# A transformer block on one core: the prologue reordered, token rows fetched ahead of expert results in the first pass

## What is computed

```
x = x + 0.5 * ffn(layernorm(x))
x = x + attn(layernorm(x))
x = x + 0.5 * ffn(layernorm(x))

ffn:  logits = t @ Wr.T + br; the two best of 8 experts; w = softmax of the two
      y = sum over the two of w * (relu(t @ W1[e].T + b1[e]) @ W2[e].T + b2[e])   # 128 -> 512 -> 128
      return layer_norm(t + y) * gamma + beta
attn: two score matrices per batch (q1 k1, q2 k2), out = (softmax(a1) - lam * softmax(a2)) @ v, then an RMS norm
```

## Time and profile before

| | |
|---|---|
| Time, median of 3 runs | 673.51 us (673.51 to 674.44) |
| The profiled execution's own time | 678.22 us |
| Its span in the trace | 676.5 us |
| TensorE busy | 596.4 us (88%) |
| VectorE, ScalarE, GpSimd busy | 452.3, 442.0, 389.7 us |
| Mean granted TensorE clock | 0.941 |

### The profile page before, as it was taken

How to read it: one execution, slowest core, us unless ns; L and a number is a source line. 1 busy time by engine, 2 the same in 40 slices (tenths; PEclk the granted TensorE clock), 3 DMA queues, 4 the chain that set the end, 5 groups by cost and what they waited for, 6 DMA issues and landing times.

```text
span 676.5 us, 16511 instructions
## 1 busy us (share of the span) xinstructions
PE 596.4 (88%) x4362; PEld 547.9 (81%) x4362; DVE 452.3 (67%) x1421; ACT 442.0 (65%) x1146; POOL 389.7 (58%) x481
## 2 busy tenths in 40 slices
PE   5988999999988759799989799897999978999945
PEld 5877999998988648688778689777999968998912
DVE  4775787445763838879968968986547553477635
ACT  4755666766656456686886786685776644887724
POOL 3006565557667178558633477585577777655623
PEclk9588999999987979999999999998999997999968
DMA  8902223223233011010000000021322423521051
GB/s 248 318 1 63 76 72 76 80 68 87 69 70 64 23 27 29 9 24 24 16 1 1 2 29 28 16 68 30 68 75 80 104 76 84 201 87 40 31 188 63
DMA packets 41881, 45.96 MB, mean 68 GB/s; under 512 B 8726, under 2 KB 32706, under 8 KB 41536
## 3 DMA queue, kind: packets, MB, share of 16 engines
q1 hardware_dynamic: 32496, 27.13, 13.7%
q0 software_dynamic: 9088, 17.75, 9.5%
q10 hardware_dynamic: 208, 0.02, 0.0%
HBM read 25.95 MB, written 19.83 MB: 68 GB/s over the span
## 4 chain that ended last, share of the span: by engine, by line
PE 53%; DVE 19%; issue 9%; POOL 8%; ACT 6%; DMA 4%; ACTq 0%; DVEq 0%; SPq 0%; POOLq 0%
PE banks L1061 18%; PE banks L1071 17%; DVE nb L1824 5%; DVE scratch L1831 3%; PE banks L1054 2%; PE banks L1158 2%; PE banks L949 2%; POOL zb L506 2%; PE banks L951 2%; PE banks L950 2%; DMA scratch<-xrows,rowbuf 2%; POOL rs L474 1%; DVE st_r L1321 1%; POOL rows L493 1%; DVE mv L1327 1%
## 5 line engine op out<-in xcount | busy, mean ns | idle before, releaser
L1061 PE MATMUL banks<-scratch 128*128 128x128 f32 x1248 | 172.9, 283 | 2.0 <-ACT scratch L695 1.0
L1071 PE MATMUL banks<-blocks,scratch 128*128 x1248 | 168.7, 279 | 3.1 <-ACT scratch L702 2.4
L1574 DVE TENSOR_SCALAR scratch<-banks,blocks 128x128 f32<-128x128 f32 x312 | 95.1, 346 | 107.4 <-PE banks L1061 97.3
L1061 PEld LDWEIGHTS banks<-scratch 128*128 128x128 f32 x1248 | 158.2, 199 | 5.5 <-issue 5.1
L1071 PEld LDWEIGHTS banks<-blocks,scratch 128*128 128x128 f32 x1248 | 154.4, 195 | 4.9 <-issue 4.5
L485 POOL DMA_INDIRECT scratch<-xrows,rowbuf x78 | 75.1, 963 | 82.0 <-DVE rowbuf L1469 42.7
L689 ACT ACTIVATE scratch<-banks 128x128 f32<-128x128 f32 x156 | 43.3, 277 | 110.1 <-PE banks L1054 108.2
L777 ACT ACTIVATE scratch<-banks,nb 128x1024 f32<-128x1024 f32 x64 | 71.3, 1116 | 50.3 <-DVE nb L1824 49.9
L517 POOL DMA_INDIRECT results<-scratch x78 | 79.4, 1018 | 37.8 <-issue 20.1
L702 ACT ACTIVATE scratch<-banks,blocks 128x128 f32<-128x128 f32 x312 | 96.7, 365 | 3.4 <-PE banks L1061 3.2
L695 ACT ACTIVATE scratch<-blocks 128x512 f32 x156 | 97.2, 623 | 0.4
(11 more groups left out here) (264 smaller groups left out, 889.0 us busy)
## 6 DMA issues: line engine op xcount, KB each, us to landing
scratch<-rows SPq DMA_DIRECT2D x78, 64.5 KB, 2.0
yrows<-scratch SPq DMA_DIRECT2D x78, 64.0 KB, 1.6
scratch<-in_L_ffn_W_dram SPq DMA_DIRECT2D x1, 2048.0 KB, 20.1
xrows<-tgt SPq DMA_DIRECT2D x4, 512.0 KB, 4.6
x<-in_L_attn_x_dram SPq DMA_DIRECT2D x3, 512.0 KB, 8.4
scratch<-xrows,rowbuf POOLq DMA_INDIRECT x78, 2.7
results<-scratch POOLq DMA_INDIRECT x78, 2.4
rows<-padrows SPq DMA_DIRECT2D x18, 64.5 KB
```

Source lines behind the costliest of these rows:

```text
L1061: ins = pe.matmul(hT_at(T, c), staged(T, c), xT_of(T), start=True, stop=True)
L1071: ins = pe.matmul(y_at(T), hT_of(T, c), blocks[:, W2_AT + c * D:][:, bass.ds(at, D)], start=(c == 0), stop=(c == FC - 1))
L1574: ins = dve.tensor_scalar(hT_of(T, c), hT_at(T, c), blocks[:, B1_AT + c:][:, bass.ds(at, 1)], 0.0, ALU.add, ALU.max)
```

## The change

Four things move; no arithmetic of the result changes.

- In the prologue VectorE copies both turned halves of batches 0 and 1 (`copy_first_turn(b, i)`, which now signals `tgtT_sb` for the second half), and ScalarE none of them. The scales of batch 1 come before the router weights, those of batch 2 behind the first logits, the statistics of batch 3 behind the choice of experts, its scales inside `pair_ids`. The table of experts and the routing weights move behind the index, into buffers `pcmp` and `peid` of their own.
- TensorE does 14 warming transposes (`warm`) and not 30. It turns the weights of experts 0 to 3 ahead of batch 3's rows and those of 4 to 7 behind them, and multiplies the token table right after that, ahead of `lam` and the query and key transposes.
- GpSimd runs `gather_x` two steps longer before it waits for written results (`WRITTEN_AT`), and then fetches the remaining rows with only three result pieces of batch 1 between them; the other 13 come behind `rstd(5)`. `rstd(6)` goes behind `ratio(0, 1)`.
- `second_merge` leaves the pass steps. Four pieces come ahead of `xm_rest(0)`, six behind `maxima(0)`, the rest behind `maxima(1)` of batch 0; what follows from it (`rstd`, the normalised `mr`, `merge_add(1)`, statistics and `xn` of batch 1) comes one query tile later.

```diff
--- before.py
+++ after.py
...
@@ -300,6 +301,7 @@
         PREFIX_AT, LOW_AT, IDS_AT = 4, 18, 23
         GATHER_AT = GSLOTS + 1
         MERGE_AT = GATHER_AT + 9
+        WRITTEN_AT = GSLOTS + 3
         MERGING = {0: 2, 1: 1, 2: 2, 3: 1} | {8 + i: 1 + i % 2 for i in range(14)}
         STATS_AT, TURN_AT = 0, 8
         CHOOSE_AT = TURN_AT + 3
@@ -530,7 +532,7 @@
             for T in range(X_AHEAD):
                 gather_x(T)
             ahead = X_AHEAD
-            for s in range(GATHER_AT):
+            for s in range(WRITTEN_AT):
                 wait_apart(pool, (xT_ps, s + 1))
                 upto = min(X_AHEAD + (s + 1) * 5 // 4, s + 1 + X_MOST)
                 for T in range(ahead, upto):
@@ -542,18 +544,18 @@
                 if i % 4 == 3:
                     gather_x(ahead)
                     ahead += 1
-            taken = 0
-            for k in range(SLOTS - ahead + PAIRS):
-                if ahead == SLOTS or k % 4 == 3:
-                    gather(1, range(taken, taken + 1))
-                    taken += 1
-                else:
-                    gather_x(ahead)
-                    ahead += 1
-                if k in (10, 22):
-                    rstd(BATCHES + k // 12)
-            assert taken == PAIRS and ahead == SLOTS
-            rstd(BATCHES + 2)
+            for T in range(ahead, ahead + 4):
+                gather_x(T)
+            gather(1, range(1))
+            for T in range(ahead + 4, ahead + 8):
+                gather_x(T)
+            rstd(BATCHES)
+            for T in range(ahead + 8, SLOTS):
+                gather_x(T)
+                if T in (ahead + 11, ahead + 14):
+                    gather(1, range((T - ahead - 8) // 3, (T - ahead - 8) // 3 + 1))
+            rstd(BATCHES + 1)
+            gather(1, range(3, PAIRS))
             all_written(1)
             gather(2, range(4))
 
@@ -573,7 +575,9 @@
                     ratio(b, i)
                     if i == TB - 1:
                         value_scale(b, 0)
-                    if after and i == (2 if b else 3):
+                    if b == 0 and i == 1:
+                        rstd(BATCHES + 2)
+                    if after and i == (2 if b else 4):
                         rstd(n)
                         n += 1
                     if last and i == 3:
@@ -788,13 +792,13 @@
                             act.wait_ge(y_written[r], sent(SLOTS, r))
                     if not after and i == TB - 1:
                         copy_tgtT(a, 1)
-                    if after and i == (0 if b else 1):
+                    if after and b and i == 0:
                         normalise(lambda j: mr[:, j * D:(j + 1) * D], mr, n - 1, halves_of(0))
                     probabilities(i, 0)
                     if i == TB - 1:
                         dT_copy(b, i - 2)
                     probabilities(i, 1)
-                    if after and i == (0 if b else 1):
+                    if after and b and i == 0:
                         normalise(lambda j: mr[:, j * D:(j + 1) * D], mr, n - 1, halves_of(1)).then_inc(scaled, 1)
                     if last and i == 0:
                         dT_copy(b - 1, TB - 1)
@@ -805,6 +809,8 @@
                         copy_v(b)
                     if 2 <= i < TB - 1:
                         dT_copy(b, i - 2)
+                    if b == 0 and i == 2:
+                        normalise(lambda j: mr[:, j * D:(j + 1) * D], mr, n - 1).then_inc(scaled, 1)
                     if 3 <= i:
                         take_o(b, i - 3)
                     if after and i == TB - 1:
...
@@ -865,22 +871,21 @@
             first_rows(0, range(2, 4), (half_rstd, 1))
             first_rows(0, halves_of(1))
             root(1, (ln_stats, 2))
-            copy_tgtT(0, 1)
             for h in range(2):
                 first_rows(1, halves_of(h))
             root(2, (ln_stats, 3))
-            copy_tgtT(1, 1)
             for h in range(2):
                 first_rows(2, halves_of(h))
-            root(3, (ln_stats, 4))
             for i in range(2):
                 copy_tgtT(2, i)
+            weights(range(E // 2))
+            root(3, (ln_stats, 4))
             for h in range(2):
                 first_rows(3, halves_of(h))
-            pair_gap(0)
             for i in range(2):
                 copy_tgtT(3, i)
-            weights(range(E))
+            weights(range(E // 2, E))
+            pair_gap(0)
             act.wait_ge(lam_ps, 1)
             act.activation(lame[:, :], bank(3, 2 * D, 2 * D + 2), ACT.Exp).then_inc(lam_exp, 1)
             n = BATCHES + 1
...
@@ -1215,7 +1220,9 @@
                 first_logits(b)
                 if b == GB:
                     pair_prefix(0)
-            weights(range(E))
+                    weights(range(E // 2))
+            weights(range(E // 2, E))
+            find_ids(0, range(4))
             pe.wait_ge(lam_in, 1)
             pe.wait_ge(w2_sb, E)
             pe.matmul(bank(3, 2 * D, 2 * D + 2), ones[:, :], lamp[:, :], start=True, stop=True).then_inc(lam_ps, 1)
@@ -1223,7 +1230,6 @@
             for m in range(4):
                 ins = pe.transpose(bank(4, m * D, (m + 1) * D), qkw[:, m * D:(m + 1) * D], ident[:, :])
             ins.then_inc(qkT_ps, 1)
-            find_ids(0, range(4))
             pe.wait_ge(w1_sb, E)
             pe.wait_ge(w2_sb, E)
             pe.wait_ge(qkT_sb, 1)
...
@@ -1839,6 +1845,8 @@
                     if after and i == TB - 1:
                         xnT_rest(b + 1)
                     if b == 0 and i == 0:
+                        at_once(itertools.islice(second_merging, 6))
+                    if b == 0 and i == 1:
                         at_once(second_merging)
                     if b > 1 and i == 0:
                         read_logits(a - 1)
@@ -1848,9 +1856,9 @@
                         add_values(b - 1, 0)
                         dve.wait_ge(ln_stats, n)
                         tile_stats(st_r, x_tile(b - 1), halves_of(0))
-                    if after and i == (1 if b else 2):
+                    if after and i == (1 if b else 3):
                         merge_add(b + 1)
-                    if after and i == (2 if b else 3):
+                    if after and i == (2 if b else 4):
                         x_stats(b + 1, n)
                         n += 1
                     if last and i == 3:
@@ -1893,38 +1901,45 @@
             shifts(0, 2, halves_of(1)).then_inc(ln_rstd, 1)
             linked(tile_stats(st_x, x_tile(1), halves_of(1)))
             aggregate(1).then_inc(ln_stats, 1)
+            shifts(1, 3).then_inc(ln_rstd, 1)
             router_weights()
-            copy_first_turn(0)
-            shifts(1, 3).then_inc(ln_rstd, 1)
+            copy_first_turn(0, 0)
+            copy_first_turn(0, 1)
             dve.wait_ge(ln_stats, 2)
             dve.wait_ge(x_loaded[2], 16)
-            linked(tile_stats(st_x, x_tile(2)))
+            tile_stats(st_x, x_tile(2), halves_of(0))
+            copy_first_turn(1, 0)
+            linked(tile_stats(st_x, x_tile(2), halves_of(1)))
+            copy_first_turn(1, 1)
             aggregate(2).then_inc(ln_stats, 1)
-            copy_first_turn(1)
-            dve.wait_ge(ln_stats, 3)
-            dve.wait_ge(x_loaded[3], 16)
-            tile_stats(st_x, x_tile(3), halves_of(0))
-            shifts(2, 4).then_inc(ln_rstd, 1)
-            linked(tile_stats(st_x, x_tile(3), halves_of(1)))
-            aggregate(3).then_inc(ln_stats, 1)
             dve.wait_ge(masks_made, 1)
             dve.tensor_copy(place_b, place_f)
             read_pair(0)
+            choosing = pair_choose(0)
+            next(choosing)
+            shifts(2, 4).then_inc(ln_rstd, 1)
+            at_once(choosing)
+            dve.wait_ge(ln_stats, 3)
+            dve.wait_ge(x_loaded[3], 16)
+            linked(tile_stats(st_x, x_tile(3)))
+            at_once(pair_place(0))
+            aggregate(3).then_inc(ln_stats, 1)
+            ids_0 = pair_ids(0)
+            next(ids_0)
+            next(ids_0)
             shifts(3, 5).then_inc(ln_rstd, 1)
-            at_once(pair_choose(0))
-            at_once(pair_place(0))
-            at_once(pair_table(0))
-            at_once(pair_ids(0))
+            at_once(ids_0)
             at_once(pair_lows())
             small_weights()
-            at_once(pair_weights(0))
+            pair_index(0)
             dve.wait_ge(qkT_ps, 1)
             dve.tensor_copy(qkwT[:, :], bank(4)).then_inc(qkT_sb, 1)
-            pair_index(0)
+            at_once(pair_table(0))
             minus_lambda()
             dve.wait_ge(M_ps, 1)
             steps.then(dve.tensor_scalar(Mh[:, :], bank(3, 0, 2 * D), SCALE, None, ALU.mult))
             dve.scalar_tensor_tensor(Ml[:, :], bank(3, 0, 2 * D), SCALE, Mh[:, :].bitcast(F32), ALU.mult, ALU.subtract).then_inc(M_sb, 1)
+            at_once(pair_weights(0))
             n = BATCHES
             first_merging, second_merging = first_merge(n), second_merge(n + 2)
```

(4 more changed lines are left out.)

17 lines of the change are left out of this document (9 added, 8 removed).

## The result

The changed kernel takes 664.32 us (median of 4 runs, 662.58 to 666.64) against 673.51 (median of 4 beside it). The ratio is 0.9868, with a 95% interval from 0.9832 to 0.9904: about 9 us faster, between 6.5 and 11.3. The profiled execution has a span of 660.8 us and took 662.58, which is 1.7 under its median; the profiled one of before was 4.7 over its own.

What follows compares the result with a forecast made beforehand. It took TensorE, half of the chain, to be held by waits for other engines, and by its own order in the prologue. Terms +5.8 - 11.3 - 7.0 = -12.5 from 673.5 gave 661.0 us, range 654.5 to 668.5.

Steps and rivals of the forecast that it cites:

- Prologue, +5.8: Prologue: batch 2's later scales delay ScalarE, `pair_place` and batch 3; first gather at 55.1 instead of 49.27, +5.8 us.
- The lower bound: Prologue: with the high clock throughout (logits 1.7, weights 3.9), first gather at 51.9, +2.6 us.
- Low clock in both first batches: Prologue: with 14 warming transposes instead of 30, TensorE idles before real work and runs both first batches at low clock.
- Pass, -11.3: Pass 0: TensorE's lost 12.1 us around waits for gathered rows go; with +2.0 and -1.2 the sum is -11.3 us.
- The 1.2 us charged to ScalarE for `rstd(5)`: Pass, step 72: ScalarE wants the scale for `xn` at about 200.4, `rstd(5)` ends at 201.6; 1.2 us charged.
- Attention, -7.0: Attention of batch 0: VectorE's waits for `cc` (10.9 us) go, less delays of 0.7, 2.4 and 0.8; -7.0 us.
- Slack of 1.8 us ahead of `ratio(0)`: Start of attention: `ratio(0)` comes 11.6 us behind the opening product, VectorE asks at 13.4; 1.8 us slack for 17 gathers.
- The merge pieces that the forecast had charged with 1.1 us each: Start of attention: some three of 17 gathers run beside merge pieces and lengthen, 3.3 us together, costing 1.5.
- Sum, -12.5: Whole kernel: prologue +5.8, pass -11.3 and attention -7.0 give -12.5 us, from 673.5 to 661.0.
- Rival A: Prologue costs next to nothing or gains, through early high clock or hidden late scales; 655 us, chance 0.15.
- Rival B: Attention's wait only moves, as `ratio(0)` or the merge pieces come as late as before; 668 us, chance 0.14.
- rival C: Slower: each of the 17 gathers takes 2.06 us, so `ratio(0)` is 17 late; 678 us, chance 0.05.

Runs made afterwards that it cites:

- both repairs: Changed kernel with batch 2's scales ahead of the first read and batch 3's statistics, scales and row normalising moved earlier: 655.99 us, ratio 0.9730 to the kernel before.

## Why the prediction was right, and where not

The forecast was 661.0 us in a range of 654.5 to 668.5 and came to 664.32; the direction and the mechanism held. By its steps:

- **Prologue, +5.8.** The chain was right link by link, and the forecast was about 1.7 us too late in each: rows of batch 2 forecast at 24.4 and seen at 22.77, `pair_place` 33.2 and 31.44, end of batch 3's logits 47.0 and 45.4, first gather 55.1 and 53.25. The offset comes from the first link: batch 1's logits were read at 21.20, not 22.9. The difference to the first gather came out nearly right by luck, since the profile of before that I counted from had the latest of eight old prologues: new ones start their first gather at 53.25, 53.11, 54.54 and 55.44, median 53.9, old ones at 47.88, so +6.0. By time the prologue alone costs 9.6 us (6.6 to 12.7), 3.8 more than forecast, though the lower end of the interval is only 0.8 above the forecast. This is the term that was mis-sized most. The lower bound was also summed wrongly: with both sets of logits at 1.7 us and the weights at 3.9 the first gather would be at 50.3, +1.0, not at 51.9, +2.6; nothing came near it.
- **Low clock in both first batches.** The granted clock was 1.00 from 8 to 14 us and 0.53 from 14 to 20, so by the record wrong for batch 0. By durations it was half right: the first four turns of batch 0 took 1.06 us, as four transposes do at 0.50, the next four 0.66. The logits of batches 2 and 3 lasted 3.42 and 3.47 as forecast.
- **Pass, -11.3.** From first turn to opening product -12.1. Tile 68 was issued at 188.22. Counted from the turn of tile 56, which stands at 168.77 here and at 163.90 in the forecast, that is 19.5 us, where 20.0 was forecast; its rows took 3.9 us until TensorE went on with them (192.12), not 2.6, and it was late by 0.41. The two errors nearly cancel. The 1.2 us charged to ScalarE for `rstd(5)` were 0.31, and that is the difference.
- **Attention, -7.0.** -8.6. The waits of 10.9 went and one of 1.98 came at `ratio(2)`, where 2.4 was forecast. ScalarE's normalising ran without a wait.
- **Slack of 1.8 us ahead of `ratio(0)`.** 2.06 by the trace, and taking it away costs what it should. Of the 17 gathers (205.99 to 226.12) the first took 1.10 us, the others 0.94 or 0.95, none 2.06. The merge pieces that the forecast had charged with 1.1 us each did stand beside them and cost nothing; the gathers that became longer stand beside a `difference`. In the timelines of VectorE and GpSimd:

```profile
217.10 1.27 DVE L1608 SCALAR_TENSOR_TENSOR scratch<-scratch,wts,tgt 128x128 f32<-128x128 f32 x4
225.49 1.25 DVE L1608 SCALAR_TENSOR_TENSOR scratch<-scratch,wts,tgt 128x128 f32<-128x128 f32 x4
...
217.39 0.94 POOL L508 DMA_INDIRECT scratch<-yrows,slot  x1 [0.30 <-issue]
231.03 1.41 POOL L508 DMA_INDIRECT zb<-yrows,slot  x1 [0.30 <-issue]
235.68 1.00 POOL L477 TENSOR_TENSOR nm<-mv,rs 128x8 f32<-128x8 f32 x1
```

The gather at 217.39 ran within four merge instructions of 0.3 us each and took 0.94. Those at 231.03 and 241.98 began inside the `difference` at 230.34 and the one at 241.85, and ended 0.83 and 0.92 us after it had ended; the small operation at 235.68, which takes 0.20 elsewhere (205.34), took 1.00 beside the one at 235.34. The Trainium skill (SBUF — State Buffer, Who interferes with whom) says that `tensor_reduce` on this chip never contends with GpSimd and an instruction with two SBUF inputs does. The trace agrees with the first (0.94 beside the maxima at 222.20) and with the second for the `difference` of 1.27 us; beside the short merge instructions, which have two such inputs too, it shows nothing of it, and no run here says why.
- **Sum, -12.5.** Pass and attention together were forecast at -18.3; the kernel with these alone has -17.1 (-14.8 to -19.5) in time and -20.3 in the trace once the first gathers are aligned (span less first gather 607.0 against 627.2 and 627.4). The prediction took a gain counted in a profile off the median, while both profiles of before seem to be 2 to 3 us longer there than its median (with the reserve made above). The forecast was 3.3 us low: 1.2 by pass and attention and 3.8 by the prologue, less the 1.7 by which the parts miss the whole.

Rival A (the prologue costs nothing) is refuted by the prologue alone at +9.6 and by the old prologue with the rest at -17.1. Rival B (attention's wait only moves) is refuted by 57.98 to 49.39. Of rival C the mechanism is seen in single gathers behind the ratios (1.41 and 2.07 us), in none of the 17.

## What to carry to other kernels

A reordering that is right in two of three places can be a loss in the third, and one number for all hides that: here one part cost 9.6 us and the others won 17.1. Time each part alone and in the company it needs. In a chain of engines the small operation to move is the one whose reader waits: the scales of two batches, under half a microsecond each, moved up in VectorE's order, and ScalarE's rows of batch 3 moved ahead of its weight copies, were together worth 6 us of first gather (the first scales alone 1.6). And before a difference is taken from one profile, profile the kernel before twice: its prologue alone moved by 2.5 us.

## What the runs showed of the hardware

The granted clock doesn't always tell at which level TensorE works. Windows of TensorE alone (busy us and count, granted clock, DMA share, GB/s), the changed kernel first, then the one with both repairs:

```profile
14.00:30.00 16.00, 12.04 (x58) 0.51 1.04 343
```

```profile
14.00:30.00 16.00, 14.22 (x65) 1.00 1.01 335
```

In both, the 16 logits of batch 2 took 3.42 us in this stretch; the 16 of batch 3 in the second kernel, at 38.74, took 1.95. So the record says 1.00, 2.4 GHz, while the durations are those seen at 0.50, 1.2 GHz. I have no run that explains it; durations of equal instructions are the safer witness.

The low clock comes where the waits are. Windows of TensorE from 186 to 222 us (end of the pass) and from 222 to 258 (attention), for four kernels: before (second profile), the changed one, the fetches alone and the merge alone:

```profile
186.00:222.00 36.00, 30.11 (x219) 0.86 0.31 68
222.00:258.00 36.00, 25.63 (x112) 0.86 0.08 21
```

```profile
186.00:222.00 36.00, 33.52 (x271) 1.00 0.37 76
222.00:258.00 36.00, 31.11 (x184) 1.00 0.11 30
```

```profile
186.00:222.00 36.00, 29.91 (x225) 1.00 0.33 69
222.00:258.00 36.00, 27.21 (x139) 0.86 0.09 25
```

```profile
186.00:222.00 36.00, 30.13 (x226) 0.91 0.32 71
222.00:258.00 36.00, 30.95 (x178) 1.00 0.10 26
```

Whoever keeps the waits of the pass has 0.86 or 0.91 in the first window, whoever keeps those of attention has 0.86 in the second, and where they are gone it is 1.00. This fits with a pass that lost 12 us while its idle rows showed under 3 each.

And one chip in these runs added 100 us to every kernel by its stops. The ratios from it agreed with the others within 0.25% for three kernels and differed by 1.2% for the fourth, the new pass and attention with the old prologue.
